# Eight edge streams in the sort and histogram, a four-deep gather ring in the segment max, and GpSimd as gatekeeper of the adjacency

## The chip, the core and the metric

The program runs on one core of one Trainium2 chip. The metric is the device time of one execution in microseconds. A core has five engines with a queue each: TensorE (PE), VectorE (DVE), ScalarE (ACT), GpSimd (POOL) and SyncE (SP). They meet only at semaphores. DMAs are issued from the queues of SP, ACT and POOL; the indirect ones (scatter or gather by a column of row numbers) come from POOL.

## What is computed

A graph of 3125 nodes and 100,000 edges, sorted by destination, goes through four layers. Cut to what matters here:

```
h = relu(layernorm(x));  x = x + L0(h)      # messages by edge type, segment_sum over dst, GRU
h = relu(layernorm(x));  x = x + L1(h)      # edge attention:
    e1, e2 = (efeat @ W_msg) * h[src],  (efeat @ W_attn) * h[src]        # [E, 16, 16]
    m = segment_max(e2, dst);  ex = exp(e2 - m[dst])
    x += segment_sum(e1 * ex / segment_sum(ex, dst)[dst], dst).sum(1)
h = relu(layernorm(x));  x = x + L2(h)      # four graph convolutions with edge weights
h = relu(layernorm(x));  x = x + L3(h)      # sheaf layer with reflections
```

The kernel makes no use of the order in which the edges come: it sorts them itself by destination block.

## The kernel before

The nodes lie in NB = 25 blocks of 128. The kernel is a chain of stages, each a `Block` with a barrier at its end, so the stages add up. Within a stage the order on each engine is the order in which the code is written; loops are `Fori` loops of the hardware, and buffers are mostly two deep, picked by `h = n % 2`.

**Sort.** The 100,000 edges lie as EP = 125 partitions by EC = 800 columns. The columns are cut into NS = 4 streams of SC = 200 columns, and one step takes one column of each stream, 4 x 125 edges. `histogram` counts edges by destination: at each step DVE makes two one-hot tiles (`hot_lo`, 128 wide for each stream, L216, and `hot_hi`, 25 wide, L218) and PE multiplies them into a count. `rank_and_scatter` then gives each edge its slot in the sorted table. Per step s, with two buffers h:

- SP loads two rows for all partitions, `key_row` and `hi_row` (L325, L326), once DVE has released the buffer (`row_used`, after `same` of step s-2).
- DVE runs `one_hots` of step s+1 (L335, L337, then L340, which needs the loaded `hi_row`), and after it `place` of step s: one `same` operation for each stream (L347, needs `key_row`), the release of the row buffer, `picked` (L353), `base` (L355), three small ones and `row_i` (L365).
- PE looks up the counters (`found`, L401) and advances them (`next_ps`, L405). ACT copies the counters (L386) and the records of the step (`staged`, L388).
- POOL waits for `staged` and `row_i` and issues one indirect DMA for each stream, 125 records each (L421), 800 in all. `staged` and `row_i` of step s wait until the DMAs of step s-2 have landed (`sent`).

**Segment max.** After the sort the edges lie in NT = 832 tiles of 128 slots. `segment_max` takes HB = 4 tiles a turn, 208 turns. POOL gathers the node rows of four tiles into `ring`, two turns deep (the helper `gather`, L1257). It waits for `idx`, four columns of row numbers that DVE copies for turn n+2 at the start of turn n (L1331), after `held` says that ACT has read the ring's half. PE turns the gathered rows (`src_ps`, L1403), ACT copies them (`src_t`, L1373; `held`, L1374), PE widens them (L1412) and forms `net` (L1417), ACT copies (`src_w`, L1379), DVE multiplies (`logit`, L1350), scans twice (`run`, L1355), makes `hot` (L1244) and folds the last turn's result into `top` (L1339). PE's order in a turn is: sources and logits of turn n+1, `back` of n (L1430), `best` of n (L1438).

**Adjacency.** `adjacency` takes NT2 = 1408 tiles, eight a turn, 176 turns. DVE makes one-hot and weighted tiles (L635 to L641, six operations); PE adds three products for each tile into PSUM at a column read from `m.table` (L679); ACT copies finished groups out and clears them (`evac`, L658 and L660). Before each tile PE waits for `evac` to reach a number that it reads from the same table; 16 numbers are loaded for a turn. POOL has nothing to do in this stage.

## Time and profile before

| | us |
|---|---|
| median of 3 runs | 8465.72 (8461.97 to 8473.73) |
| the profiled execution | 8461.1 |
| its span, first to last instruction | 8459.0 |
| histogram, 112 to 282 | 170 |
| sort with the histogram's tail, 282 to 1663 | 1381 |
| segment max, 2935 to 4131 | 1196 |
| adjacency, 5500 to 6130 | 630 |

The stages are read off the timeline by the first and last instruction of their lines. Of the span, DVE is busy 73%, PE 69%, POOL 53% and ACT 19%, but no engine is the limit all the way: the stages have different ones. In the rows below, "idle before" is the time that the engine waited ahead of an instruction, and the arrow names what it waited for; "issue" is waiting for nothing that the profile shows.

### The profile page before, as it was taken

Reading aid. Unit: us, or ns where it says so; the run is one execution under the profiler, and the core shown is the slowest. Engines: PE = TensorE matmul, PEld = TensorE weight load, DVE = VectorE, ACT = ScalarE, POOL = GpSimd, SP = SyncE. Lnnn points to the kernel's source line nnn. Section 1 sums busy time; section 2 is a strip of 40 time slices with the busy share of each in tenths; the row PEclk is TensorE's granted clock in tenths of the full one; section 3 lists DMA queues with packets and bytes.
Section 4 is the critical chain, followed back from the end, with each engine's and each line's share of the span. In section 5 each row is a group of like instructions: output and inputs, shape, how many; then the busy total and the mean of one; then the engine's idle time right before and its main releaser. Section 6 shows DMA issues by size and latency. Waiting matters only on the chain. (4 is left out here: it accounts for less than half of the span.)

```text
span 8459.0 us, 123102 instructions
## 1 busy us (share of the span) xinstructions
PE 5854.0 (69%) x33625; PEld 3950.5 (47%) x33626; DVE 6136.2 (73%) x12788; ACT 1635.2 (19%) x2872; POOL 4450.0 (53%) x4142
## 2 busy tenths in 40 slices
PE   3433333347444477777699999466559699999999
PEld 1333333236444455555455555255424366666555
DVE  5766666547333399999899999889900188888898
ACT  0011111001010144444222222034100022222000
POOL 0377767567777577777477777300000177777100
PEclk9999999955555599999899999677879755555899
DMA  2122222233111233333411111022065311111000
GB/s 97 32 52 53 52 51 52 43 108 70 38 36 38 37 79 80 80 80 79 54 44 43 43 44 43 13 94 99 31 253 205 148 31 32 32 32 32 3 0 1
DMA packets 487779, 514.79 MB, mean 61 GB/s; under 512 B 259365, under 2 KB 389805, under 8 KB 477106
## 3 DMA queue, kind: packets, MB, share of 16 engines
q1 hardware_dynamic: 344198, 446.65, 16.9%
q0 software_dynamic: 132160, 43.97, 6.5%
q10 hardware_dynamic: 11232, 21.73, 0.8%
q8 instruction: 109, 1.79, 0.1%
q14 instruction: 80, 0.66, 0.0%
HBM read 415.02 MB, written 95.99 MB: 60 GB/s over the span
## 5 line engine op out<-in xcount | busy, mean ns | idle before, releaser
L1257 POOL DMA_INDIRECT sh_ring<-node,sh_idx x832 | 856.8, 1030 | 1535.4 <-DVE sh_idx L1895 1277.6
L421 POOL DMA_INDIRECT slots<-rank_staged,rank_row_i x800 | 952.0, 1190 | 414.7 <-issue 210.1
L1507 POOL DMA_INDIRECT slots<-sm_rec,sm_row x832 | 900.9, 1083 | 361.8 <-issue 208.8
L1257 POOL DMA_INDIRECT mx_ring<-node,mx_idx x832 | 861.1, 1035 | 398.2 <-issue 239.5
L919 POOL DMA_INDIRECT mid_ring<-typed,mid_idx x832 | 873.5, 1050 | 258.7 <-issue 253.2
L401 PE MATMUL rank_found<-rank_next_sb,rank_hot_hi_t 25*125 25x128 f32 x1600 | 407.3, 431 | 840.3 <-ACT rank_next_sb L386 825.0
L1617 PE MATMUL sm_sums<-sm_both,sm_hot 128*128 128x512 f32 x1664 | 787.1, 595 | 0.4 <-issue 0.2
L401 PEld LDWEIGHTS rank_found<-rank_next_sb,rank_hot_hi_t 25*125 25x125 f32 x1600 | 353.6, 321 | 890.3 <-DVE rank_hot_hi_t L340 890.3
L1124 PE MATMUL mid_sums<-mid_ring,mid_hot_d 128*128 128x17 f32 x1664 | 391.7, 375 | 455.9 <-DMA mid_ring<-typed,mid_idx 443.5
L1124 PEld LDWEIGHTS mid_sums<-mid_ring,mid_hot_d 128*128 128x128 f32 x1664 | 383.3, 312 | 472.6 <-issue 472.6
L2135 PE MATMUL srl_sums<-srl_outer,srl_hot_lo 128*128 128x400 f32 x1664 | 560.9, 500 | 7.4 <-DVE srl_outer L2117 7.4
L679 PE MATMUL adj_sums<-adj_heavy,adj_hot 128*128 128x128 bf16 x4224 | 378.8, 253 | 234.9 <-issue 87.8
L1355 DVE TENSOR_TENSOR_SCAN mx_run<-mx_far,mx_run,mx_logit 128x512 f32<-128x512 f32 x414 | 509.1, 1271 | 21.5
L1438 PE MATMUL mx_best<-mx_run_e,mx_hot 128*128 128x256 f32 x1664 | 422.1, 397 | 48.4 <-ACT mx_run_e L1388 48.0
L679 PEld LDWEIGHTS adj_sums<-adj_heavy,adj_hot 128*128 128x128 bf16 x4224 | 313.9, 114 | 301.2 <-issue 272.4
L2135 PEld LDWEIGHTS srl_sums<-srl_outer,srl_hot_lo 128*128 128x128 f32 x1664 | 316.9, 191 | 252.3 <-DVE srl_outer L2117 9.1
L2035 PE MATMUL sh_hid_ps<-sh_ends_t,mlp 32*128 32x512 f32 x416 | 392.9, 1096 | 54.5 <-ACT sh_ends_t L1988 54.5
L1575 ACT ACTIVATE sm_both<-sm_net_a 128x512 f32<-128x512 f32 x416 | 248.5, 597 | 938.4 <-PE sm_net_a L1604 938.4
L340 DVE TENSOR_SCALAR rank_hot_hi_t<-rank_hi_row,iota_col 25x500 f32<-25x500 f32 x200 | 117.2, 586 | 401.2 <-DMA rank_hi_row<-hi_rows 401.2
L1037 DVE COPY mid_ring<-fields 128x8 f32<-128x8 f32 x104 | 18.9, 181 | 501.7 <-PE mid_sums L1126 501.7
L1617 PEld LDWEIGHTS sm_sums<-sm_both,sm_hot 128*128 128x128 f32 x1664 | 283.3, 190 | 209.8 <-issue 200.8
L1681 DVE TENSOR_TENSOR agg<-c_sums,dinv_row 128x3200 f32<-128x3200 f32 x4 | 14.0, 3492 | 502.3 <-PEq L1720 502.3
(403 smaller groups left out, 13634.0 us busy)
## 6 DMA issues: line engine op xcount, KB each, us to landing
strips<-near SPq DMA_DIRECT2D x76, 1600.0 KB, 10.8
mx_far<-far_row SPq DMA_DIRECT2D x208, 256.0 KB
rank_key_row<-key_rows SPq DMA_DIRECT2D x200, 244.1 KB
near<-adj_whole SPq DMA_DIRECT2D x175, 256.0 KB, 2.0
sm_low<-low_row SPq DMA_DIRECT2D x208, 128.0 KB
sh_low<-low_row SPq DMA_DIRECT2D x104, 256.0 KB, 3.3
feat_t<-mid_out ACTq DMA_DIRECT2D x104, 204.0 KB
mx_feat<-feat_t SPq DMA_DIRECT2D x208, 102.0 KB
```

The lines of the kernel that those rows point to most:

```text
L401: last = nc.tensor.matmul(found[h][:, j, :], hot_hi_t[:, h, j, :], next_sb[:, h, j * P:(j + 1) * P], start=True, stop=True, skip_group_che ...
L421: pool.indirect_dma_start(m.slots, bass.IndirectOffsetOnAxis(ap=row_i[:, h, j:j + 1], axis=0), staged[:, h, j, :], None).then_inc(sent[h], 16)
L679: last = nc.tensor.matmul(sums[:, bass.ds(at[2 * j], P)], hot[:, h, j // 2, :, j % 2], heavy[:, h, k, j // 2, :, j % 2], start=False, stop ...
L919: pool.indirect_dma_start(ring[:, n % DEEP, j, 0:D], None, m.typed, bass.IndirectOffsetOnAxis(ap=idx[:, t:t + 1], axis=0)).then_inc(gather ...
L1124: nc.tensor.matmul(sums[:, bass.ds(blocks[j // 2] * K17, K17)], hot_d[:, h, j, :], ring[:, n % DEEP, j, 0:K17], start=False, stop=True, sk ...
L1257: pool.indirect_dma_start(ring[:, h, j, :], None, table, bass.IndirectOffsetOnAxis(ap=idx[:, h, j:j + 1], axis=0)).then_inc(part, 16)
L1355: last = nc.vector.tensor_tensor_scan(run[:, h, c, :], far[:, h, :], logit[:, c, :], before, ALU.add, ALU.max)
L1438: last = nc.tensor.matmul(best[:, k, :], hot[:, h, 2 * k + j, :], run_e[:, h, 2 * k + j, :], start=j == 0, stop=j == 1, skip_group_check=True)
L1507: pool.indirect_dma_start(m.slots2, bass.IndirectOffsetOnAxis(ap=row2[:, t:t + 1], axis=0), rec2[:, t, :], None).then_inc(ordered, 16)
L1617: last = nc.tensor.matmul(sums[r % 2][:, :], hot[:, h, 2 * (r % 2) + j, :], both[:, r % 2, j].rearrange("q a c -> q (a c)"), start=j == 0, ...
L2035: nc.tensor.matmul(hid_ps[:, c:c + 512], m.mlp1[:, :], ends_t[:, c:c + 512], start=True, stop=True).then_inc(hp_s, 1)
L2135: last = nc.tensor.matmul(sums[:, 0:NB * D], hot_lo[:, h, j, :], outer[:, h, j, :], start=False, stop=True, skip_group_check=True)
```

## The change

NS goes from 4 to 8, so a step of the histogram and the sort takes 8 x 125 edges and there are 100 steps. In `segment_max` the ring is four turns deep, the row numbers of all tiles are copied once, POOL's loop is written out and waits for `held` of turn n-4, and the loops of ACT and PE have bodies of four turns. In `adjacency` POOL reads the `evac` numbers, waits for them and counts tiles free on a new semaphore `freed`; PE waits for that and loads only the eight columns. The table is split into two rows for it.

```
-NS = 4
+NS = 8
...
-                dve.wait_ge(sent[h], i * 64 + 16)
+                dve.wait_ge(sent[h], i * 16 * NS + 16)
...
+        @block.gpsimd
+        def _(pool):
+            def turn(q, h):
+                n = 2 * q + h
+                _, cleared_by = nc.values_load_multi_w_load_instructions(
+                    m.table[0:1, 1, bass.ds(n * BT, BT)], engines=[mybir.EngineType.Pool], min_val=0,
+                    max_val=(NB - 1) * (WIDTH_SLOTS + 1), skip_runtime_bounds_check_because=COUNTED)
+                for j in range(BT):
+                    pool.wait_ge(evac, cleared_by[j] & 511)
+                    pool.sem_inc(freed, 1)
+
+            batches(pool, total, 1, 1, turn)
...
-                    pe.wait_ge(evac, at[2 * j + 1] & 511)
+                    pe.wait_ge(freed, n * BT + j + 1)
...
+    DEEP = 4
-        idx, ring = sb("idx", [P, 2, HB], I32), sb("ring", [P, 2, HB, W40])
+        idx, ring = sb("idx", [P, NT], I32), sb("ring", [P, DEEP, HB, W40])
...
-            gather(nc, m, pool, m.node40, idx, ring, idx_s, gathered, HB, HT // 2)
+            pool.wait_ge(idx_s, 1)
+            for n in range(HT):
+                if n >= DEEP:
+                    pool.wait_ge(held, n - DEEP + 1)
+                for j in range(HB):
+                    t = n * HB + j
+                    pool.indirect_dma_start(ring[:, n % DEEP, j, :], None, m.node40,
+                                            bass.IndirectOffsetOnAxis(ap=idx[:, t:t + 1], axis=0)).then_inc(gathered[n % DEEP], 16)
...
-                if inside(n + 2):
-
-                    dve.wait_ge(held, n + 1)
-                    indices(n + 2, h)
...
+            nc.vector.tensor_copy(idx[:, :], m.fields[:, :, SRC]).then_inc(idx_s, 1)
             nc.vector.memset(m.top[:, :, :], 0.0).then_inc(cleared, 1)
```

What the program issues at the places in question follows. First the loop body of POOL in the sort, two steps; `rec_in` stands for `staged`, `at_row` for `row_i`.

```order
-L421 DMA slots<-rank_staged,rank_row_i 106496x24 [waits rank_rec_in0,rank_at_row0]
-L421 DMA slots<-rank_staged,rank_row_i 106496x24 x3
-L421 DMA slots<-rank_staged,rank_row_i 106496x24 [waits rank_rec_in1,rank_at_row1]
-L421 DMA slots<-rank_staged,rank_row_i 106496x24 x3
...
+L424 DMA slots<-rank_staged,rank_row_i 106496x24 [waits rank_rec_in0,rank_at_row0]
+L424 DMA slots<-rank_staged,rank_row_i 106496x24 x7
+L424 DMA slots<-rank_staged,rank_row_i 106496x24 [waits rank_rec_in1,rank_at_row1]
+L424 DMA slots<-rank_staged,rank_row_i 106496x24 x7
```

Between two waits POOL now has eight indirect DMAs to issue and not four; their number over the sort stays 800.

Second, DVE at the start of a turn of the segment max, before (semaphores are named here by the first stage that used their slot: `rank_sent0` is `held`, `hist_used_d0` is `run_s`, `hist_step` and `hist_counted` are `net_s` and `src_w_s`):

```order
L1331 ISA [waits rank_sent0]
L1331 COPY mx_idx<-fields 128x4
L1240 REGISTER_ALU [waits hist_step,hist_counted]
L1350 TENSOR_TENSOR mx_logit<-mx_net,mx_src_w 128x1024 [waits hist_used_d0]
L1351 ISA
L1355 SCALAR_TENSOR_TENSOR mx_run<-mx_far,mx_run,mx_logit 128x512 [waits hist_used_d1,rec_keys]
```

and now (`hist_used_d0` and `hist_used_d1` are `net_s` and `src_w_s`, `hist_hot_d0` is `run_s`):

```order
L1267 REGISTER_ALU [waits hist_used_d1,hist_used_d0]
L1378 TENSOR_TENSOR mx_logit<-mx_net,mx_src_w 128x1024 [waits hist_hot_d0]
L1379 ISA
L1383 SCALAR_TENSOR_TENSOR mx_run<-mx_far,mx_run,mx_logit 128x512 [waits hist_hot_d1,rec_feat_in]
L1383 SCALAR_TENSOR_TENSOR mx_run<-mx_far,mx_run,mx_logit 128x512
```

The copy and its wait for `held` are gone from the turn, and nothing else moved.

Third, PE in a turn of the adjacency, before (`hist_used_d0` is `hot_s`, `hist_counted` is `evac`):

```order
L672 TENSOR_LOAD table
L675 REGISTER_ALU
L677 REGISTER_ALU [waits hist_used_d0]
L679 ISA [waits hist_counted]
L679 MATMUL adj_sums<-adj_heavy,adj_hot 128x128 x3
```

and what POOL does now in a turn (`hist_used_d0` is here `evac`):

```order
L673 TENSOR_LOAD table
L677 REGISTER_ALU
L677 REGISTER_ALU [waits hist_used_d0] x7
L1241 REGISTER_ALU [waits hist_used_d0]
```

POOL has some ten instructions a turn, and a wait ahead of each tile. On PE the count stays the same: a register operation, a wait and three matmuls a tile, the wait now on `freed`.

## Rows read from the trace of the kernel before

**Rows 1.** Busy time by stage: window, length, PE, PEld, DVE, ACT, POOL, PEclk, DMA share, GB/s.

```profile
112.00:282.00 170.00, 121.92 (x802) 66.28 (x802) 165.82 (x403) 0.00 (x0) 0.00 (x0) 1.00 0.00 0
282.00:1663.00 1381.00, 519.46 (x2410) 421.04 (x2410) 883.90 (x3418) 159.39 (x400) 953.21 (x802) 1.00 0.24 51
2935.00:4131.00 1196.00, 922.94 (x4958) 598.61 (x4958) 1064.88 (x1446) 569.63 (x1035) 861.10 (x832) 0.98 0.37 77
5500.00:6130.00 630.00, 392.76 (x4240) 319.04 (x4240) 576.31 (x1065) 202.25 (x350) 0.00 (x0) 0.81 0.19 75
```

**Rows 2.** Timeline, DVE in the histogram: start, duration, engine, line, operation.

```profile
200.13 0.69 DVE L216 TENSOR_TENSOR hist_hot_lo<-lo_f,iota_row 125x512 bf16<-125x512 f32 x1
201.80 0.69 DVE L216 TENSOR_TENSOR hist_hot_lo<-lo_f,iota_row 125x512 bf16<-125x512 f32 x1
```

**Rows 3.** Groups by line, a one-hot of twice the width: busy us, mean ns, idle before.

```profile
L1038 DVE TENSOR_TENSOR mid_hot_s<-mid_lo,iota_row 128x1024 bf16<-128x1024 bf16 x104 | 126.8, 1219 | 0.0
```

**Rows 4.** Timeline of one sort step, with the idle time and its releaser.

```profile
804.01 1.18 POOL L421 DMA_INDIRECT slots<-rank_staged,rank_row_i  x1 [1.39 <-DVE rank_row_i L365]
...
807.04 0.33 DVE L347 SCALAR_TENSOR_TENSOR rank_same<-rank_key_row,key_f,below 125x125 f32<-125x125 f32 x1
...
812.51 0.64 DVE L340 TENSOR_SCALAR rank_hot_hi_t<-rank_hi_row,iota_col 25x500 f32<-25x500 f32 x1 [1.93 <-DMA rank_hi_row<-hi_rows]
```

**Rows 5.** Half a microsecond of a row load in the sort (columns as rows 1).

```profile
804.00:804.50 0.50, 0.00 (x0) 0.00 (x0) 0.00 (x0) 0.00 (x0) 0.49 (x1) 1.00 0.36 106
```

**Rows 6.** Waits of the sort stage: us in total, times, longest.

```profile
DVE rank_hot_hi_t L340 <- DMA rank_hi_row<-hi_rows: 401.2, 200, 4.7
POOL slots L421 <- DVE rank_row_i L365: 181.4, 134, 2.1
```

**Rows 7.** The scatter: its group, and its min/median/max ns with first and last start.

```profile
L421 POOL DMA_INDIRECT slots<-rank_staged,rank_row_i x800 | 952.0, 1190 | 414.7 <-issue 210.1 <-DVE rank_row_i L365 181.4 <-ACT rank_staged L388 23.1
...
L421 POOL DMA_INDIRECT slots<-rank_staged,rank_row_i x800: 1172/1178/1339, 308.3 to 1659.5; - x160
```

**Rows 8.** Timeline of the segment max, from one pair of turns.

```profile
3501.06 0.38 PE L1403 MATMUL mx_src_ps<-ident_bf,mx_ring 128*48 128x128 bf16 x4 [0.34 <-DMA mx_ring<-node,mx_idx]
...
3504.93 0.94 POOL L1257 DMA_INDIRECT mx_ring<-node,mx_idx  x1 [0.78 <-DVE mx_idx L1331]
3505.45 2.46 DVE L1355 TENSOR_TENSOR_SCAN mx_run<-mx_far,mx_run,mx_logit 128x512 f32<-128x512 f32 x2
3506.17 1.31 POOL L1257 DMA_INDIRECT mx_ring<-node,mx_idx  x1 [0.31 <-issue]
...
3506.43 0.38 PE L1403 MATMUL mx_src_ps<-ident_bf,mx_ring 128*48 128x128 bf16 x4
...
3512.24 0.38 PE L1403 MATMUL mx_src_ps<-ident_bf,mx_ring 128*48 128x128 bf16 x4 [0.50 <-DMA mx_ring<-node,mx_idx]
```

**Rows 9.** The gather and the transposes of its rows: group; then min/median/max ns, first and last start.

```profile
L1257 POOL DMA_INDIRECT mx_ring<-node,mx_idx x832 | 861.1, 1035 | 398.2 <-issue 239.5 <-DVE mx_idx L1331 158.7
...
L1257 POOL DMA_INDIRECT mx_ring<-node,mx_idx x832: 938/944/1947, 2935.2 to 4121.2; - x167
...
L1403 PE MATMUL mx_src_ps<-ident_bf,mx_ring x832: 216/218/314, 2941.5 to 4129.5; 128*48 128x128 bf16 x167
```

**Rows 10.** Ten microseconds near the end of the segment max (columns as rows 1).

```profile
4090.00:4100.00 10.00, 5.85 (x24) 3.87 (x24) 7.03 (x11) 2.91 (x5) 5.64 (x6) 0.83 0.93 48
```

**Rows 11.** Adjacency, 30 us beside ACT's evictions and 30 us without (columns as rows 1).

```profile
5560.00:5590.00 30.00, 18.89 (x213) 15.84 (x211) 28.12 (x53) 13.83 (x24) 0.00 (x0) 0.82 0.25 96
...
6040.00:6070.00 30.00, 16.66 (x221) 12.54 (x219) 28.85 (x55) 0.00 (x0) 0.00 (x0) 1.00 0.00 0
```

**Rows 12.** Waits of the adjacency: us in total, times, longest.

```profile
PE adj_sums L679 <- issue: 87.8, 70, 2.3
PE adj_sums L679 <- ACT adj_sums L660: 78.4, 57, 2.1
...
DVE adj_now L635 <- PE adj_sums L679: 35.1, 72, 1.2
```

More of the change, by code:

```diff
@@ L261, in _ @@
                                     ALU.min).then_inc(step, 1)
-            dve.wait_ge(step, 17)
+            dve.wait_ge(step, 13 + NS)
             nc.vector.tensor_copy(m.pair[:, :], blk_f[:, :].rearrange("o (t a) -> o t a", a=2)[:, :, 0])
@@ L285, in _ @@
             nc.tensor.matmul(small[:, 64:64 + NB], tot[:, :], m.ident[0:NB, 0:NB], start=True, stop=True).then_inc(mm, 1)
-            pe.wait_ge(step, 16)
+            pe.wait_ge(step, 12 + NS)
             h = NT // 2
@@ L391, in _ @@
         def _(pe):
-            nc.tensor.matmul(next_ps[:, :], m.ident[0:NB, 0:NB], m.first[:, :, :].rearrange("p j l -> p (j l)"),
-                             start=True, stop=True, skip_group_check=True).then_inc(seeded, 1)
+            firsts = m.first[:, :, :].rearrange("p j l -> p (j l)")
+            for c in range(0, NS * P, 512):
+                last = nc.tensor.matmul(next_ps[:, c:c + 512], m.ident[0:NB, 0:NB], firsts[:, c:c + 512], start=True, stop=True,
+                                        skip_group_check=True)
+            last.then_inc(seeded, 1)
             for h in range(2):
@@ L423, in _ @@
             for h in range(2):
-                pool.wait_ge(sent[h], turns * 64 + 16)
+                pool.wait_ge(sent[h], turns * 16 * NS + 16)
 def weights(nc, a, m):
@@ L587, in adjacency @@
         sums = ps("sums", [P, 8 * 512])
-        names = ("rec_in", "step", "now_s", "near_s", "hot_s", "done", "evac", "copied", "cleared")
-        rec_in, step, now_s, near_s, hot_s, done, evac, copied, cleared = map(sem, names)
+        names = ("rec_in", "step", "now_s", "near_s", "hot_s", "done", "evac", "copied", "cleared", "freed")
+        rec_in, step, now_s, near_s, hot_s, done, evac, copied, cleared, freed = map(sem, names)
         saved = [sem(f"saved{k}") for k in range(GROUPS)]
@@ L672, in turn @@
                 _, at = nc.values_load_multi_w_load_instructions(
-                    m.table[0:1, bass.ds(n * BT, BT), :].rearrange("o t k -> o (t k)"), engines=[mybir.EngineType.PE], min_val=0,
+                    m.table[0:1, 0, bass.ds(n * BT, BT)], engines=[mybir.EngineType.PE], min_val=0,
                     max_val=(WIDTH_SLOTS - 1) * P, skip_runtime_bounds_check_because=COUNTED)
@@ L676, in turn @@
                 for j in range(BT):
-                    pe.wait_ge(evac, at[2 * j + 1] & 511)
+                    pe.wait_ge(freed, n * BT + j + 1)
                     for k in range(3):
-                        last = nc.tensor.matmul(sums[:, bass.ds(at[2 * j], P)], hot[:, h, j // 2, :, j % 2], heavy[:, h, k, j // 2, :, j % 2], start=False,
+                        last = nc.tensor.matmul(sums[:, bass.ds(at[j], P)], hot[:, h, j // 2, :, j % 2], heavy[:, h, k, j // 2, :, j % 2], start=False,
                                                 stop=True, skip_group_check=True)
@@ L1229, in batches, with fours @@
         body(n // 2, n % 2)
+def fours(eng, total, body):
+    for j in range(4):
+        body(0, j)
+    with eng.Fori(0, total - 2) as i:
+        for j in range(4):
+            body(i + 1, j)
+    for j in range(4):
+        body(total - 1, j)
 def inside(n, total=HT):
@@ L1302, in segment_max @@
         back, best = [ps("back0", [P, 2, 256]), ps("back1", [P, 2, 256])], ps("best", [P, 2, 256])
-        gathered, loaded = [[sem("gathered0")], [sem("gathered1")]], [sem("loaded0"), sem("loaded1")]
+        gathered, loaded = [sem(f"gathered{k}") for k in range(DEEP)], [sem("loaded0"), sem("loaded1")]
         names = ("idx_s", "src_s", "src_t_s", "wide_s", "src_w_s", "net_s", "logit_s", "run_s", "back_s", "run_e_s", "hot_s",
@@ L1359, in turn @@
                     keep(n - 1)
+            nc.vector.tensor_copy(idx[:, :], m.fields[:, :, SRC]).then_inc(idx_s, 1)
             nc.vector.memset(m.top[:, :, :], 0.0).then_inc(cleared, 1)
             dve.wait_ge(cleared, 1)
-            for h in range(2):
-                indices(h, h)
             batches(dve, HT, 3, 3, turn)
@@ L1369, in _, with sources @@
         def _(act):
-            def sources(q, h):
-                n = 2 * q + h
+            def sources(n, k):
                 act.wait_ge(src_s, n + 1)
-                nc.scalar.copy(src_t[:, h], src_ps[:, :]).then_inc(src_t_s, 1)
-                nc.scalar.copy(m.held[:, bass.ds(n * HB, HB), :], ring[:, h, :, 0:D]).then_inc(held, 1)
+                nc.scalar.copy(src_t[:, k % 2], src_ps[:, :]).then_inc(src_t_s, 1)
+                nc.scalar.copy(m.held[:, bass.ds(n * HB, HB), :], ring[:, k, :, 0:D]).then_inc(held, 1)
             def widened(n):
@@ L1391, in _, with sources @@
             widened(0)
[L1392 removed]
+            fours(act, HT // 4, turn)
         @block.tensor
         def _(pe):
[L1396 to L1399 removed]
+            def sources(q, k):
+                n = 4 * q + k
+                pe.wait_ge(gathered[k], (q + 1) * 16 * HB)
                 wait(pe, src_t_s, n)
@@ L1413, in logits @@
                 last.then_inc(wide_s, 1)
-                pe.wait_ge(loaded[h], (q + 1) * 32)
+                pe.wait_ge(loaded[h], (2 * q + k // 2 + 1) * 32)
                 wait(pe, logit_s, n)
@@ L1443, in _ @@
             logits(0, 0)
-            batches(pe, HT, 1, 1, turn)
+            fours(pe, HT // 4, turn)
 def split_top(nc, m):
@@ L2244, in build @@
             rb = on(scope)
-            m.table, m.marks = rb("table", [1, NT2, 2], I32), rb("marks", [1, NB, 8], I32)
+            m.table, m.marks = rb("table", [1, 2, NT2], I32), rb("marks", [1, NB, 8], I32)
             bucket_table(nc, m)
```

36 lines of the change are left out of this document (15 added, 21 removed).

## The prediction, made before the run

> **What bounds the kernel now.** First the busy time by stage [rows 1], because the engines' shares of the whole span average over stages with different limits. The change touches four stages: histogram (170 us), sort (1381), segment max (1196) and adjacency (630). The others are left as they are, and barriers stand between stages, so what a stage gains the kernel gains.
>
> *Histogram.* DVE is busy 165.8 of 170 us: it is the bound. Two steps take 201.80 - 200.13 = 1.67 us [rows 2].
>
> *Sort.* No engine is full; POOL, with 953 of 1381 us, is nearest. So the waits. POOL waits 181 us for `row_i`, and DVE waits 401 us, at all 200 steps, for the loaded `hi_row` [rows 6]. One step shows the loop [rows 4]: the last `same` ends at 807.37 and releases the row buffer, SP loads the rows anew, `hi_row` is there at 812.51 (5.14 us after the release, 1.93 us of it plain waiting on DVE), `hot_hi_t` takes up to 0.64, four `same` follow at 0.27 each, and the buffer is released again: 5.14 + 0.5 + 1.1 = 6.7 us a step. 1351 us from the first scatter to the last [rows 7] over 200 steps are 6.76. This loop is the bound, with POOL close behind: four scatters at 1.19 us and 0.3 us before each (1.19 is the mean [rows 7], 0.3 is what stands before an indirect DMA that waits for nothing [rows 8]) are 5.96.
>
> *Segment max.* DVE is busy 1065 of 1196 us, PE 923. Here the engines wait for each other in turn. PE starts its turns at 3501.06, 3506.43 and 3512.24: 5.37 us to a start that waits for nothing, 5.81 to one that waits 0.50 for the gather, whose POOL waited 0.78 for DVE's `idx` [rows 8]. The whole stage runs at (4129.4 - 2941.5)/207 = 5.74 a turn [rows 9], more than the 5.6 of such a pair, because POOL now and then needs 1.9 us for a gather in place of 0.94 [rows 9] and because near the end the DMA engines are 93% busy at a mere 48 GB/s [rows 10].
>
> *Adjacency.* DVE is busy 576 of 630 us. It makes 53 operations (8.8 turns) in 30 us beside ACT's evictions and 55 (9.2 turns) without them [rows 11]: DVE is the bound, and loses 35 us to a late PE, which lost 78 us to ACT [rows 12].
>
> **Histogram, part by part.** 100 steps of twice the width. A one-hot of 512 takes 0.69 [rows 2], one of 1024 1.22 [rows 3]: 0.53 more. `hot_hi` grows by 100 elements, by the same rate 0.10. A step is then 0.84 + 0.53 + 0.10 = 1.47, the stage 147 us in place of 167: **-20**. Its tail has wider operations and four more additions, and the seeding product is doubled: I charge **+4**, from 0 to 8; that work stands alone, so nothing hides it.
>
> **Sort.** The number of scatters stays at 800, and their cost on POOL too. What changes is what a round trip of the row load pays for: eight scatters, not four. Two limits compete.
> POOL: 8 x 1.49 = 11.9 us a step.
> The loop of the row load: 586 KB in place of 293. While it runs the DMA shows 106 GB/s at a share of 0.36 [rows 5], so the added 293 KB cost 2.8 us: 5.14 + 2.8 = 7.9, plus `hot_hi_t` 0.5 to 0.9 and eight `same` 2.2, is 10.6 to 11.0. The DVE work that lies beside the load (picked, base, small ones, two one-hots, about 4.6) is covered. That is under POOL's 11.9, by 1 us. ACT and PE round trips grow to some 7 us and are covered too, and `sent` of step s-2 comes some 8 us before POOL wants step s.
> So POOL becomes the bound: 799 x 1.49 = 1191 in place of 1351: -160. Two limits that lie so near disturb each other a little: +3 (none to 10). The first scatter comes later: two row loads in a row, each 2.9 longer, and the wider chain behind them (same 1.1, picked and base 0.5 each): +8. Sum **-149**.
> Ends: 1.48 a scatter, -157. At the other end the load's whole 5.14 doubles, not its data part alone (a rival, below).
>
> **Segment max.** The `idx` copy, its wait and POOL's wait for it go; nothing of it comes back but one copy of 832 numbers ahead of the stage. Next is PE's own chain: 5.37 a turn [rows 8]. POOL needs 4 x 1.035 + 4 x 0.29 = 5.29 [rows 9], now without a partner to wait for: almost as much. I take 5.42. Gathers of 1.9 us vanish in a ring three turns ahead. Near the end the DMA engines stay full, which a ring can't change; of some nine turns at 6.9 I keep 8 us over 5.42, and 2 for the first turns at PE's lower clock. 207 x 5.42 + 10 = 1132 against 1188: -56. POOL also starts 5 us earlier, as `idx` is copied before the memset of `top` and not after: -4 net of the longer copy. **-60**; with 5.37 a turn -70, with 5.6 (a rival) -23. POOL's loop written out means no other cost that a row shows: the ends of the turns in its present loop cost the same 0.3.
>
> **Adjacency.** PE keeps its count of instructions and loads 8 numbers, not 16. That saves at most a part of its 88 us of "issue" [rows 12], and PE is not the bound. Each tile for which PE waited for ACT now has a hand-over through POOL on the way. The trace has no POOL instruction in this stage, so bounds: below, 35 us, all that DVE waits for PE, if a lighter PE made it good; above, POOL's whole 0.78 us before a gather that waited for `idx` [rows 8], which holds the waiting itself, at each of PE's 57 waits for ACT [rows 12], 45 us. A semaphore alone is nearer to the bottom; 0.15 us each is **+8**.
>
> **Sum**: -20 + 4 - 149 - 60 + 8 = **-217**. 8461.1 - 217 = 8244 for an execution like the profiled one, which lies 4.6 under the median: **8248**. What is hidden or small (table split, ACT's wider copies) I cost at nothing: in each case the engine has over a third of the stage idle.
>
> **Rivals.**
> *The row load stays the bound.* If issue and landing grow with the size as well, 10.3 + 0.8 + 2.2 = 13.3 us a step, 1330 for the sort: -13 for -149, total 8384. For it: SP's row loads come from rows of 500 bytes, and DMA engines are shared with a denser scatter. Against: the load's fixed part. Partly so (12.3 a step): 8285.
> *POOL and DVE collide in the segment max.* Inside a scan of 1.2 us a gather took 1.31 in place of 0.94 [rows 8], others up to 1.95. Today POOL's start is tied to DVE's `idx`, before the scans; untied, a gather may begin anywhere in them. Half a scan lost a turn: 4 x 1.25 + 0.6 = 5.6, -23 for -60: 8285. A whole scan, 6.2, would be +101 for -60, 8409.
> The Trainium skill, "SBUF — State Buffer", "Who interferes with whom", says that a DVE operation with two inputs in SBUF and a GpSimd operation that reads SBUF exclude each other for the whole instruction. The 1.31 agrees in kind; by that rule at its hardest the whole-scan figure would hold.
> *The kernel gets slower: POOL paces the adjacency.* POOL has eight waits, eight register operations and a load a turn. If each costs the 0.3 us that stand before POOL's DMAs, a turn is 17 x 0.3 = 5.1 us in place of 3.5, 176 turns +280 for +8: total 8520. It decides from 3.5/17 = 0.2 us an instruction. Against: POOL's waits at step ends in the sort cost nothing over the 0.3.
> *The change does nothing* in the sort, because POOL's pace is not 1.49 when DVE never idles: it would need 1.69 a scatter, above all but a few; the longest is 1.34 [rows 7].
>
> **Chances.** Forecast (8215 to 8280) 0.62; collision in the segment max 0.17; row load, wholly or partly, 0.13; slower 0.03; better than the forecast, with a gain in the adjacency too, 0.05. The range takes in the bounds of the segment max, the partial row load, and a gain of 20 in the adjacency: 8195 to 8325. A difference of 0.2% (17 us) is about what a measurement can tell. Faster 0.95, same 0.02, slower 0.03.
>
> **What would show it.** Histogram: DVE's `hot_lo` every 1.47 us. Sort: POOL's wait for `row_i` near zero, 1.5 us from scatter to scatter, DVE waiting for `hi_row` still but without anyone waiting for DVE. Segment max: no gather waits for `idx`; the transposes every 5.4 us; PE's wait for the gather small. If POOL's mean gather is over 1.1 us and PE waits for the ring, the collision is real. Adjacency: DVE's wait for PE at 35 us or a little more; POOL well ahead. The prediction is wrong if POOL still waits for `row_i` at most steps, or if the adjacency grows by more than 50 us.

## The result, and the profile after

| | before | after |
|---|---|---|
| median us | 8463.84 (8461.23 to 8473.73, 4 runs) | 8240.52 (8215.09 to 8245.35, 4 runs) |
| span of the profiled execution | 8459.0 | 8242.4 |
| histogram | 170 | 149 |
| sort with the histogram's tail | 1381 | 1280 |
| segment max | 1196 | 1149 |
| adjacency | 630 | 583 |

The ratio is 0.9728, with a 95% interval of 0.9706 to 0.9750: 223 us by the medians, 217 by the two spans. The four stages give 21 + 101 + 47 + 47 = 216, so the rest of the kernel did not move. The forecast was 8248. The total is almost exact, but two of its terms are off by 44 and 55 us in opposite directions, and that is what the experiments are about.

The stages after (window, length, PE, PEld, DVE, ACT, POOL, PEclk, DMA share, GB/s); they answer to [rows 1]:

```profile
112.00:261.00 149.00, 106.40 (x804) 76.54 (x804) 145.10 (x205) 0.00 (x0) 0.00 (x0) 1.00 0.00 0
261.00:1541.00 1280.00, 477.53 (x2412) 424.62 (x2412) 759.43 (x2520) 128.59 (x200) 999.91 (x802) 1.00 0.26 55
2811.00:3960.00 1149.00, 913.24 (x4962) 592.96 (x4963) 1040.73 (x1241) 575.69 (x1036) 857.84 (x832) 0.98 0.39 81
5329.00:5912.00 583.00, 336.62 (x4240) 249.96 (x4240) 567.71 (x1064) 201.52 (x350) 0.00 (x0) 0.98 0.21 81
```

**Histogram.** Timeline of DVE, against [rows 2]:

```profile
199.55 1.22 DVE L216 TENSOR_TENSOR hist_hot_lo<-lo_f,iota_row 125x1024 bf16<-125x1024 f32 x1
200.68 0.35 DVE L218 TENSOR_TENSOR hist_hot_hi<-hi_f,iota_row 125x200 bf16<-125x200 f32 x1
200.96 1.22 DVE L216 TENSOR_TENSOR hist_hot_lo<-lo_f,iota_row 125x1024 bf16<-125x1024 f32 x1
```

A step takes 200.96 - 199.55 = 1.41 us, over the stage 1.43.

**Sort.** The scatter's group and its smallest, median and longest duration, against [rows 7], and below them two waits of the stage, against [rows 6]:

```profile
L424 POOL DMA_INDIRECT slots<-rank_staged,rank_row_i x800 | 998.7, 1248 | 265.5 <-issue 260.0 <-ACT rank_staged L388 3.7 <-DVE rank_row_i L365 1.8
...
L424 POOL DMA_INDIRECT slots<-rank_staged,rank_row_i x800: 1175/1184/2410, 295.1 to 1536.1; - x160
```

```profile
DVE rank_row_i L365 <- DMA slots<-rank_staged,rank_row_i: 308.7, 78, 5.2
DVE rank_hot_hi_t L340 <- DMA rank_hi_row<-hi_rows: 101.1, 31, 8.9
```

POOL waits 1.8 us for `row_i` in place of 181, and but for 5.5 us all of its idle time is "issue": POOL is the bound, as forecast. Scattering takes 1536.1 - 295.1 = 1241 us, 110 less than before. But the mean scatter has grown from 1190 to 1248 ns, while the median has hardly moved; 74 of the 800 take over 1.5 us, the longest 2.41. The timeline shows which:

```profile
901.08 1.18 POOL L424 DMA_INDIRECT slots<-rank_staged,rank_row_i  x1 [0.30 <-issue]
902.22 0.17 DVE L365 SCALAR_TENSOR_TENSOR rank_row_i<-rank_pos 125x8 int32<-125x8 int32 x1 [5.10 <-DMA slots<-rank_staged,rank_row_i]
902.34 1.23 DVE L335 TENSOR_TENSOR rank_hot_lo<-lo_f,iota_row 125x1024 bf16<-125x1024 f32 x1
902.57 2.26 POOL L424 DMA_INDIRECT slots<-rank_staged,rank_row_i  x1 [0.30 <-issue]
...
905.14 1.21 POOL L424 DMA_INDIRECT slots<-rank_staged,rank_row_i  x1 [0.31 <-issue]
```

A scatter that begins at 902.57, inside `hot_lo` (902.34 to 903.57), ends 2.26 us later and not 1.18. Counted over the stage, 88 scatters begin inside `hot_lo`, with a mean of 1.73 us, and 73 of the 77 that take over 1.4 us are among them. The earlier in `hot_lo` a scatter begins, the longer it takes: 2.29 us on the mean at 0.1 to 0.2 us after its start, 1.53 at 0.9 to 1.0. So it waits for `hot_lo` to end, and ends itself 1.05 to 1.27 us later. (The eight that begin in its first 0.03 us take 1.18 and don't wait.) They meet so often because something ties them: DVE waits 5.10 us for the landing of an earlier scatter, then writes `row_i` and goes straight on to `hot_lo`, in the rhythm of the scatters.

In the kernel before, 96 scatters begin inside `hot_lo` too, but each in its last 0.15 us, and they take 1.18 us:

```profile
809.72 0.69 DVE L335 TENSOR_TENSOR rank_hot_lo<-lo_f,iota_row 125x512 bf16<-125x512 f32 x1 [0.34 <-issue]
810.28 1.18 POOL L421 DMA_INDIRECT slots<-rank_staged,rank_row_i  x1 [0.63 <-issue]
```

**Segment max.** The transposes run from 2818.9 to 3957.9, 1139.0 us against 1188 [rows 9]. Gather and pace in 800 us of the middle (3019 to 3819), and under it the end of the stage (the columns of the windows as above):

```profile
L1360 POOL DMA_INDIRECT mx_ring<-node,mx_idx x600 | 617.8, 1030 | 182.9 <-issue 180.5 <-ACT held L1400 2.4
```

```profile
3820.00:3880.00 60.00, 49.29 (x272) 32.30 (x270) 56.27 (x68) 30.56 (x56) 45.97 (x47) 1.00 0.38 87
3880.00:3920.00 40.00, 26.98 (x125) 17.39 (x124) 28.20 (x35) 14.85 (x27) 30.21 (x29) 0.83 0.88 54
3920.00:3958.00 38.00, 20.38 (x96) 13.69 (x96) 17.86 (x22) 10.74 (x19) 3.78 (x4) 0.78 0.59 48
```

600 gathers in 800 us are 1.33 us each, 5.33 a turn, and that is just a gather (1.030) and what stands before it (0.30): POOL has hardly any other idle time (2.4 us) and sets the pace. Then the end: 78 us in which PE does 221 matmuls. At the pace of the 60 us before (272) that is 49 us. The DMA engines are 88% busy there with less to move than before.

**Adjacency.** The products run from 5344.9 to 5909.4, 564.5 us; before it was 5517.1 to 6128.0, 610.9. Its waits, against [rows 12]:

```profile
PE adj_sums L695 <- DVE adj_heavy L644: 129.1, 93, 2.1
PE adj_sums L695 <- POOLq L678: 114.9, 83, 1.6
```

DVE has no wait for PE left (35.1 us before), PE waits for DVE. A turn takes (5904.6 - 5341.5)/175 = 3.22 us, which is DVE's own work, and the granted clock is 0.98 where it was 0.81 [rows 1].

### The profile page after: what moved, and what is told of

It is laid out like the page before. It is cut to its first block and busy times, and to the rows that moved or that the text cites. A ratio compares the mean times of both kernels' runs of the same rounds, so it can differ in the third digit from the quotient of the medians.

```text
span 8242.4 us, 120531 instructions
## 1 busy us (share of the span) xinstructions
PE 5734.8 (70%) x33629; PEld 3891.4 (47%) x33630; DVE 5955.1 (72%) x11485; ACT 1609.0 (20%) x2672; POOL 4496.5 (55%) x4143
## 3 DMA queue, kind: packets, MB, share of 16 engines
q8 instruction: 111, 1.82, 0.1%
## 5 line engine op out<-in xcount | busy, mean ns | idle before, releaser
L424 POOL DMA_INDIRECT slots<-rank_staged,rank_row_i x800 | 998.7, 1248 | 265.5 <-issue 260.0
L404 PE MATMUL rank_found<-rank_next_sb,rank_hot_hi_t 25*125 25x128 f32 x1600 | 374.3, 422 | 764.0 <-ACT rank_next_sb L386 748.5
L695 PE MATMUL adj_sums<-adj_heavy,adj_hot 128*128 128x128 bf16 x4224 | 322.7, 222 | 244.0 <-DVE adj_heavy L644 129.1
L695 PEld LDWEIGHTS adj_sums<-adj_heavy,adj_hot 128*128 128x128 bf16 x4224 | 245.0, 98 | 323.2 <-issue 275.5
L2068 PE MATMUL sh_v_ps<-mlp,sh_hid 128*128 128x32 f32 x1664 | 374.5, 401 | 0.0
```

Of the source, the lines that this page charges most:

```text
L404: last = nc.tensor.matmul(found[h][:, j, :], hot_hi_t[:, h, j, :], next_sb[:, h, j * P:(j + 1) * P], start=True, stop=True, skip_group_che ...
L424: pool.indirect_dma_start(m.slots, bass.IndirectOffsetOnAxis(ap=row_i[:, h, j:j + 1], axis=0), staged[:, h, j, :], None).then_inc(sent[h], 16)
L695: last = nc.tensor.matmul(sums[:, bass.ds(at[j], P)], hot[:, h, j // 2, :, j % 2], heavy[:, h, k, j // 2, :, j % 2], start=False, stop=Tru ...
```

## The experiments

`e1` to `e4` ran on a chip where the kernel before takes 9395 us, `e9` and `e10` on one where it takes 9419, and `e5` to `e8` on one where it takes 8450, close to the first comparison. On the first two, engines stop in the segment max and other stages for "issue" and "remote", up to 10.8 us at a time; what makes them is not resolved. Ratios are therefore taken within a batch, and stages are compared by their rows. The old products of the adjacency span 610.7 to 611.3 us in `before`, `e1` and `e5`. The scatters of the unchanged eight-stream sort vary more: 1241.0 us after the change, 1241.7 in `e1`, 1239.5 in `e3`, 1236.6 in `e8` and 1224.8 in `e6`.

### Which edit brings what

`e1_sort_only` and `e2_adjacency_only` take one part of the change each over into the kernel before; `e5_ring_only` takes the third.

```
 e1:  -NS = 4          +NS = 8
 e2:  bucket_table and adjacency of the change
      -rb("table", [1, NT2, 2], I32)   +rb("table", [1, 2, NT2], I32)
 e5:  segment_max of the change
```

> The kernel before with eight streams in the histogram and the sort, and nothing else of the change. If the stages are independent, histogram and sort take what they take in the changed kernel: the one-hot every 1.43 us, 1241 us from the first scatter to the last, and the other stages stay as before; total about 8464 - 25 - 110 + 13 (the later last scatter is in these) = 8340 +- 10. If part of the gain of the changed kernel elsewhere came from the sort (another order of the slots), segment max or adjacency move by over 5 us.

> The kernel before with the adjacency of the change (POOL reads the evac numbers and hands tiles to PE by freed; PE loads eight numbers a turn) and nothing else. If the 46 us there come from this edit: products from first to last 565 us and not 611, DVE waits for PE for nothing, granted clock in the stage 0.98 and not 0.81, total about 8418. If they come from the other stages (a denser program ahead, another clock history), the stage stays at 611 and the total at 8464.

> Only the four-deep ring of the segment max is taken over into the kernel before; histogram, sort and adjacency stay at four streams and at the old release. My theory: the stage is set by VectorE at about 5.3 to 5.4 us a turn, and the deeper ring takes the waits for a landed gather away; on a chip like the one of the first two traces the row of the turned gathers would span 1139 us in place of 1188, the ratio would be 0.994 and the other stages would not move. Rival (collision): if GpSimd's gathers had grown beside VectorE's two-operand work, their mean would be over 1.1 us and the stage would not shorten; the trace of the changed kernel shows 1031 ns, so I expect this to fail. Second rival: where the landings are slower, as in the four experiments before, the ring is used up by the landings, and the stage is set by them before and after: ratio 0.985 to 1.0 with gather waits left on TensorE or on GpSimd's hold.

| | ratio | 95% interval | the stage |
|---|---|---|---|
| e1 | 0.9895 | 0.9857 to 0.9933 | scatters span 1241.7 us, mean 1249 ns, as after |
| e2 | 0.9938 | 0.9916 to 0.9961 | products 564.5 us, as after |
| e5 | 0.9950 | 0.9935 to 0.9966 | transposes 1165.4 us, after 1139.0 |

The adjacency in `e2`, 584 us of its trace, and its waits:

```profile
6142.00:6726.00 584.00, 336.81 (x4240) 250.00 (x4240) 567.71 (x1064) 201.41 (x350) 0.00 (x0) 0.98 0.21 81
```

```profile
PE adj_sums L692 <- DVE adj_heavy L641: 127.7, 93, 1.5
PE adj_sums L692 <- POOLq L675: 116.7, 83, 2.5
```

Both agree with the changed kernel to within 2 us: the 46 us in the adjacency come from its own edit and from nothing else in the change. So do the long scatters from the eight streams. The expectation of `e5` failed: the ring alone is worth half of what its stage gained, 22.5 us of 49. The three ratios multiply to 0.978 where the whole change has 0.973; half of that gap is the 26 us that the ring lacks here, the rest lies within the intervals. Its gathers in the middle of the stage:

```profile
L1344 POOL DMA_INDIRECT mx_ring<-node,mx_idx x580 | 624.5, 1077 | 176.7 <-issue 176.7
```

1.077 + 0.30 four times is 5.51 a turn, against 5.33. POOL paces the stage here too, with the same ring, but its gathers are 4% longer. In the changed kernel three of a turn's four take 0.95 us and one 1.13 to 1.61:

```profile
3301.91 2.46 DVE L1383 TENSOR_TENSOR_SCAN mx_run<-mx_far,mx_run,mx_logit 128x512 f32<-128x512 f32 x2
3302.57 1.38 POOL L1360 DMA_INDIRECT mx_ring<-node,mx_idx  x1 [0.30 <-issue]
```

and in `e5` one at the same place takes 1.79:

```profile
3302.24 2.46 DVE L1367 TENSOR_TENSOR_SCAN mx_run<-mx_far,mx_run,mx_logit 128x512 f32<-128x512 f32 x2
3302.49 1.79 POOL L1344 DMA_INDIRECT mx_ring<-node,mx_idx  x1 [0.30 <-issue]
```

How far a scan has got when the gather begins decides its length. The two scans shown together as x2 start 1.20 us apart. After the change the first ends at 3303.20, the gather at 3303.95; in `e5` the scan ends at 3303.53, the gather at 3304.28. So it is for all of them: the 150 long gathers of the 800 us after the change, the 144 of `e5` and the 135 of the kernel before all begin inside a scan (a DVE operation with both inputs in SBUF) and end 0.75 us after it, where the others take 0.95 in all. They begin 0.77 us into the first scan after the change (median) and 0.55 us in `e5`. The gathers cost 0.34 and 0.53 us a turn by this, and 4 x (0.944 + 0.30) = 4.98 and these make the two paces, 5.33 and 5.51. Why the same code settles at one distance with eight streams and at another with four wasn't tried, and stays open.

### The long scatters of the sort

`e4_iota_in_psum`: the changed kernel, in which ACT copies the counting row to PSUM once and both one-hots of the sort compare against the copy. DVE does the same work in the same time, with one of its two inputs outside SBUF.

```
+        iota_ps, iota_s = ps("iota_ps", [EP, P]), sem("iota_s")
...
-                 m.iota_row[0:EP, None, :].to_broadcast([EP, NS, P]), ALU.is_equal)
+                 iota_ps[:, None, :].to_broadcast([EP, NS, P]), ALU.is_equal)
...
+            nc.scalar.copy(iota_ps[:, :], m.iota_row[0:EP, :]).then_inc(iota_s, 1)
```

> The changed kernel, with the row of column numbers that the sort's one-hots are compared against held in PSUM and not in SBUF, so that these two operations of DVE read one operand from SBUF and one from PSUM. Theory A, DVE shuts POOL out while it reads two operands from SBUF: the scatters of 2.3 us beside the wide one-hot (1.23 us) vanish, the mean scatter falls from 1.25 to about 1.20 us, the sort from 1241 to about 1200 us, total about 8200. Theory B, the long scatter comes from the DMA side (it starts as the last scatter of two steps before lands): nothing changes.

Ratio 0.9668 (0.9633 to 0.9703); `e3`, which ran beside it and has the sort of the changed kernel, has 0.9779. Of the 105 us between the two medians only 40 are the scatters (1239.5 and 1199.6 us); 63 are the slower adjacency of `e3`. Scatter group and durations, and the place that was long before:

```profile
L427 POOL DMA_INDIRECT slots<-rank_staged,rank_row_i x800 | 957.3, 1197 | 264.6 <-issue 257.9 <-ACT rank_staged L391 5.2 <-DVE rank_row_i L366 1.5
...
L427 POOL DMA_INDIRECT slots<-rank_staged,rank_row_i x800: 1175/1181/1653, 294.3 to 1493.9; - x160
```

```profile
899.15 1.22 DVE L336 TENSOR_TENSOR rank_hot_lo<-lo_f,rank_iota_ps 125x1024 bf16<-125x1024 f32 x1 [0.35 <-issue]
899.32 1.18 POOL L427 DMA_INDIRECT slots<-rank_staged,rank_row_i  x1 [0.30 <-ACT rank_staged L391]
```

The scatter again begins inside `hot_lo`, which takes 1.22 us as it did, and now takes 1.18; so do all 80 that begin inside it (mean 1.18, in place of 1.73). The mean of all is down from 1248 to 1197 ns, no scatter is over 1.65 us, and the scatters span 1199.6 us in place of 1241. DVE still waits for the landings as it did (262 us here, 309 there), so it is the second input in SBUF that holds POOL up, and not the landing or the load of the DMA engines. The stage's gain in `e4`, `e7` and `e10` (1197 to 1200 us) against the five spans above is 25 to 44 us. The Trainium skill, "SBUF — State Buffer", "Who interferes with whom", says that a DVE operation with two SBUF inputs and a GpSimd operation that reads SBUF exclude each other, and that one with a single SBUF input does not contend: this pair of runs agrees with both halves, with 2.26 and 1.18 us. The same section infers that a `tensor_tensor` does not stall GpSimd's issue of DMAs; `hot_lo` is one, and the 2.26 us say that it does, so the measurement decides.

### What slowed the adjacency before

The change does two things to PE there: it loads 8 numbers a turn in place of 16, and it waits for a constant in place of a register's value. Its count of instructions is the same. `e3_load_sixteen` puts the table and PE's load back and keeps the hand-over through POOL, whose own load is then of every second number. `e8_wide_load` was meant to leave POOL's load alone and to widen only PE's, and its expectation says so. But the kernel that ran as `e8` is line for line that of `e3`: it is a repetition on another chip, and it separates nothing.

```
 e3 and e8
     -m.table[0:1, 1, bass.ds(n * BT, BT)]      (POOL)
     +m.table[0:1, bass.ds(n * BT, BT), 1]
...
     -m.table[0:1, 0, bass.ds(n * BT, BT)]      (PE)
     +m.table[0:1, bass.ds(n * BT, BT), :].rearrange("o t k -> o (t k)")
```

> The changed kernel, but the table is laid out as before and PE loads all sixteen numbers of a turn again, of which it uses eight; POOL still does the waiting. Theory A, PE's sequencer: the time that PE needs between two bursts is mostly this load (1.27 us of idle before a burst at full clock before, with DVE's operands ready); with sixteen numbers it comes back, the stage goes to 595 to 612 us and the granted clock falls. Theory B, the waits: PE was held up by waits whose number came out of a register loaded from the table; these stay with POOL, so the stage stays at 565.

> The changed kernel; only TensorE's sequencer loads 16 numbers a turn of the adjacency products, the 8 it needs and GpSimd's 8, and uses the first 8. GpSimd's own load stays as it is, a row of 8 that lie together. Theory A (the width of TensorE's load was the second bound of the stage before): the products span 600 us or more in place of 564.5, TensorE starts its bursts 1 us or more after its operands are ready, and its clock falls below 0.9. Theory B (the width costs nothing; the experiment with the interleaved table was slow for GpSimd's load of every second number, and the kernel before for its 8 waits against a register): 560 to 570 us, clock 1.0, as in the changed kernel.

`e3` has a ratio of 0.9779 (0.9751 to 0.9808), `e8` 0.9813 (0.9793 to 0.9833). The products take 627.9 and 629.6 us, more than `e3`'s theory A allowed (595 to 612) and more than the 611 of the kernel before. The stage in `e8`, then its waits:

```profile
5321.50:5967.00 645.50, 399.51 (x4238) 326.17 (x4239) 578.08 (x1064) 201.59 (x348) 0.00 (x0) 0.78 0.19 73
```

```profile
PE adj_sums L695 <- POOLq L678: 242.0, 173, 2.4
DVE adj_now L638 <- PE adj_sums L695: 53.3, 103, 1.7
...
PE adj_sums L695 <- DVE adj_heavy L644: 4.0, 3, 2.0
```

The wait booked on "POOLq" is real here. The trace also keeps a record of each sequencer's loads and semaphore instructions, which the views shown leave out. POOL's load of eight numbers takes 0.57 us in the changed kernel (0.66 on the mean) when they lie side by side, and 1.82 us or more (2.02 on the mean) when they are every second one. With the eight hand-overs at 0.16 us each and the loop's own instructions that makes a turn of POOL 3.60 us in `e8`, and in it POOL stands still for an `evac` once, for 0.5 us. In 101 of 174 turns PE starts its first tile within 0.05 us of POOL's release. So `e3` and `e8` are slow because POOL paces the stage, and they can't tell what PE's load costs. In the changed kernel POOL's release lies at least 3 us ahead of PE's first tile in every turn, and there the 83 waits booked on POOLq are not waits for POOL.

What slowed the stage before is in the same records. A turn of PE's sequencer in its parts, means in us:

| | before | after | e8 | e9 |
|---|---|---|---|---|
| load from the table | 1.24 | 0.67 | 1.25 | 0.66 |
| from there to the first tile's matmuls | 0.26 | 0.63 | 0.37 | 0.36 |
| first to eighth tile | 1.50 | 1.49 | 1.50 | 2.87 |
| from there to the next load | 0.49 | 0.43 | 0.48 | 0.53 |
| turn | 3.48 | 3.22 | 3.59 | 4.42 |

Before, none of the 174 turns holds a wait of over 0.04 us for DVE's operands, and the eight waits for `evac` cost next to nothing: the first to eighth tile take 1.50 us against a register, 1.49 against a constant. PE's sequencer is always busy, and its 3.48 us are the stage's turn. The waits that the profile books there on ACT [rows 12] are its sequencer's. The change takes 0.57 us out of the load; 0.38 us of it come back as waiting for DVE, whose turn of 3.22 is now the bound. So it is the width of the load (theory A), shown by `before`, `e2` and the changed kernel, and the register waits (theory B) are out. A load of 16 numbers takes 1.11 us where nothing is evicted and 1.29 on the mean beside evictions; one of 8, 0.59 and 0.69.

A timeline shows the same from the side of the matmuls. Before, without an eviction near:

```profile
6042.69 1.85 PE L679 MATMUL adj_sums<-adj_heavy,adj_hot 128*128 128x128 bf16 x24 [1.27 <-issue]
6046.26 1.83 PE L679 MATMUL adj_sums<-adj_heavy,adj_hot 128*128 128x128 bf16 x24 [1.72 <-issue]
6049.38 1.83 PE L679 MATMUL adj_sums<-adj_heavy,adj_hot 128*128 128x128 bf16 x24 [1.28 <-issue]
```

after:

```profile
5853.43 1.85 PE L695 MATMUL adj_sums<-adj_heavy,adj_hot 128*128 128x128 bf16 x24 [1.39 <-DVE adj_heavy L644]
5856.65 1.81 PE L695 MATMUL adj_sums<-adj_heavy,adj_hot 128*128 128x128 bf16 x24 [1.37 <-DVE adj_heavy L644]
```

Before, the starts are 3.57 and 3.12 us apart, 3.35 on the mean, and PE waits for nothing but its own sequencer. DVE's turn of 3.22 lies below that: PE was the bound, by a little. After, the starts are 3.22 apart, and it is DVE's `heavy` that ends the wait. Beside the evictions the longer loads add to the 3.35. The longer turn goes with a lower granted clock. A hundred microseconds beside the evictions, of `e8` and of the changed kernel:

```profile
5420.00:5520.00 100.00, 62.61 (x663) 52.95 (x660) 88.47 (x164) 41.90 (x73) 0.00 (x0) 0.74 0.24 94
```

```profile
5430.00:5530.00 100.00, 56.93 (x750) 43.13 (x749) 98.95 (x187) 46.44 (x81) 0.00 (x0) 1.00 0.27 105
```

The clock is 0.74 against 1.00, and DVE makes 164 operations against 187. In `e8` a burst takes 2.74 us in place of 1.83 where the clock is low:

```profile
5890.96 2.74 PE L695 MATMUL adj_sums<-adj_heavy,adj_hot 128*128 128x128 bf16 x24 [1.71 <-POOLq L678]
5894.20 1.83 PE L695 MATMUL adj_sums<-adj_heavy,adj_hot 128*128 128x128 bf16 x24 [0.50 <-POOLq L678]
```

The longer burst is not what makes the turn long: PE's sequencer goes from the first to the eighth tile in 1.50 us at a clock of 0.78 and in 1.49 at 0.98, and the burst of 2.74 is followed by the next after 0.50 us.

If only the width counts, the relay through POOL isn't needed: `e9_packed_before` puts address and count of a tile in one number, and PE takes them apart.

```
-                    pe.wait_ge(evac, at[2 * j + 1] & 511)
+                    pe.wait_ge(evac, (at[j] >> 12) & 511)
...
-    last = nc.tensor.matmul(sums[:, bass.ds(at[2 * j], P)], ...
+    last = nc.tensor.matmul(sums[:, bass.ds(at[j] & 3968, P)], ...
```

> The kernel before, and only the adjacency's table is another: address and evacuation count of a tile stand in one number, so TensorE loads 8 numbers a turn in place of 16 and takes them apart with two further register instructions a tile (16 a turn). There is no relay through GpSimd; TensorE waits against a register as before. Theory (the width of the load is what costs, about 65 us over 176 turns, 0.37 us a turn): the products go from 611 to 565 to 580 us, TensorE's clock in the stage goes above 0.9, and the ratio is 0.994 to 0.997, as with the relay. Rival (the relief came from the wait against a constant in place of one against a register, or the register instructions cost as much as the loads): the products stay at 605 us or more and the ratio is 0.999 to 1.001.

The ratio is 1.0155 (1.0133 to 1.0177), slower than before, and the products take 775.8 us. Two of its turns:

```profile
6603.04 3.35 PE L680 MATMUL adj_sums<-adj_heavy,adj_hot 128*128 128x128 bf16 x24 [0.96 <-ACT adj_sums L661]
6607.58 3.38 PE L680 MATMUL adj_sums<-adj_heavy,adj_hot 128*128 128x128 bf16 x24 [1.19 <-ACT adj_sums L661]
```

The theory missed; the rival had the direction (605 us or more), but not the size. The load is as narrow as in the change, but two more register instructions a tile, 0.10 us each, stretch the burst itself to 3.35 us, beyond even the 2.74 of the low clock: 4.41 us a turn, with DVE waiting for PE in 174 turns (193 us). Over the first 620 us of the stage the granted clock is 0.52, for the most part the lower of the two levels (1.2 GHz):

```profile
6180.00:6800.00 620.00, 467.89 (x3337) 262.00 (x3335) 459.62 (x842) 203.01 (x348) 0.00 (x0) 0.52 0.19 74
```

So here PE's sequencer, not its array, sets the pace, as it did before the change: 16 register instructions more cost 0.93 us a turn, although 8 numbers fewer are loaded. The hand-over through POOL is good for exactly this: it takes eight numbers off PE's sequencer and puts nothing on it. It pays only with the table split, so that POOL's numbers too lie side by side.

### The slow end of the segment max

`e6_spread_holes`: unused slots of the sorted list name spread rows; in the changed kernel they all name row 0.

```
+ nc.vector.tensor_scalar(hv[:, :, FIELDS + SRC], m.iota_col[:, 0:1].to_broadcast([P, 32]), 24.0, None, ALU.mult).then_inc(hole_s, 1)
+ nc.vector.tensor_scalar(hv[:, :, FIELDS + TIX], m.iota_col[:, 0:1].to_broadcast([P, 32]), 192.0, None, ALU.mult).then_inc(hole_s, 1)
```

> The changed kernel, but an unused slot of the sorted list names a source row of its own partition (24 times the partition's number, and the type index likewise) and not row 0. Unused slots weigh nothing, so the output does not change; the gathers of the last turns read 128 different rows where they read one row 128 times. My theory: the slow end of the segment max (3880 to 3958 in the changed kernel: 78 us for work that takes 49 us at the pace ahead of it, DMA share 0.88 at 54 GB/s against 0.38 at 87) is the price of reading one address many times. Then the stage ends about 30 us earlier, the DMA share in its last 80 us is that of the stretch ahead, and the total falls by 25 to 60 us against the changed kernel, since other passes gather the same slots. Rival: the slow end belongs to other transfers that start there; then nothing moves, and the tail keeps its share of over 0.8.

The transposes take 1110.0 us, 29 less than in the changed kernel, as expected. The ratio is 0.9710 (0.9682 to 0.9739); against the 0.9728 of the changed kernel the intervals overlap, so the gain in the total isn't resolved, and by the stage it is 29 us and not up to 60. Its sort was 16 us shorter as well, with the same code: 59 scatters of over 1.4 us in place of 77. The last 77 us:

```profile
3825.00:3865.00 40.00, 33.07 (x182) 21.55 (x180) 37.56 (x46) 20.37 (x38) 30.86 (x31) 1.00 0.36 88
3865.00:3902.00 37.00, 30.14 (x165) 19.69 (x166) 34.82 (x43) 19.33 (x35) 26.12 (x26) 1.00 0.32 84
```

The DMA share stays at 0.32 to 0.36, and the longest gather from issue to landing is 4.2 us, where it was 19.0 (10.4 before the change, and 17.0 in `e5` with the deeper ring alone; that more gathers in flight make the difference is an inference). What I had taken in the prediction for full DMA engines, which a ring can't help, was many reads of one row.

### Together

`e7_both` has both edits on top of the change; `e10_packed_both` is `e7` with the packed table for the relay.

> The changed kernel with two edits at once: the sort's one-hots compare against a copy of the counting row in PSUM, and the unused slots name spread rows. If the two act in different stages they add up: the sort's scatters span 1200 us in place of 1241, and the segment max loses its slow end; about 70 us under the changed kernel, ratio to the kernel before 0.963 to 0.966 if the chip is as the one of the first four experiments, 0.964 on one like the first. If the spread rows do nothing, this kernel equals the one with the copy in PSUM alone (0.967).

> The kernel with the counting row in PSUM and the spread unused slots (0.9648 of before), with the packed table of the run above in place of GpSimd's relay. If packing does all that the relay does, the products take 565 us again and the ratio stays 0.963 to 0.967. If the relay is also worth something by itself (a wait less on TensorE's sequencer), the products take 575 us or more and the ratio is 0.966 or higher. VectorE's own work sets 3.21 us a turn either way, so neither can bring the stage under 560 us.

`e7`: 8150.74 us (8150.44 to 8152.82, 4 runs), ratio 0.9648 (0.9632 to 0.9664), the best of all. Its scatters span 1198.3 us, its transposes 1107.0. The two add up, as they act in different stages. `e10`: 0.9877 (0.9858 to 0.9897), with products of 775.8 us as in `e9`. The second expectation (575 us or more) holds, but not for its reason, a wait less on PE: it is the register instructions again.

## Why the prediction came out right, point by point

- **Histogram, -20 + 4.** A step takes 1.43 where 1.47 was worked out; 0.04 over 100 steps is the difference. The stage lost 21 us, and of the tail's +4 nothing shows apart in the sort's window.
- **Sort, -149: right in mechanism, too large.** POOL is the bound, the row load is covered: `hi_row` is still waited for in 31 of 100 steps, but no scatter waits for it, so the rival "row load stays the bound" is out. The term that was mis-sized is "799 x 1.49 = 1191": 1.49 rests on 1.19 a scatter [rows 7], measured where the scatters that began inside `hot_lo` began in its last 0.15 us, and where `hot_lo` was 0.69 us long and not 1.23. Measured 1.248 + 0.30, 1241 us. 800 x 0.058 = 46 us are what the collision costs, and `e4` gives 41 of them back against the changed kernel. The rule was on the table, as a rival for the segment max; it belonged at every place where the change lets POOL run freely beside a two-input operation of DVE. The first scatter, put at +8, came 13 us earlier, since the histogram ahead of it is 21 shorter: relative to that it is 8 later, as said.
- **Segment max, -60.** Measured -49 in the row of transposes, -47 in the stage. The pace was better than the 5.42 taken, 5.33, and the limit is POOL's 5.29 of the text, not PE's 5.37. The collision of the rival is real and was there all along: one gather a turn waits for a scan, in the kernel before as after, and its price stood already in the mean of 1.035 [rows 9]. It is 0.34 us a turn after the change and 0.53 in `e5`, where the rival charged 0.6 and the forecast nothing more. That the distance to the scan did not shrink with the untied ring is luck: nothing in the prediction says where it would settle. The stated sign (a mean gather of over 1.1 us) could not see it. The end was worse: it cost 29 us over the pace where 8 were kept, and `e6` shows why.
- **Adjacency, +8: wrong sign.** Measured -46. The failed step is "PE is not the bound": it was read from DVE's busy share and from the 35 us that DVE waits. But an undisturbed DVE turn is 3.22 us, and the stage ran at (6122.2 - 5513.5)/175 = 3.48; a stage bound by DVE would have run at 3.22. What set the pace was PE's sequencer, with a load of 1.24 us in each turn. The lower end of the term, 35 us, was the wait of DVE alone, and the real gain lies beyond it. The 57 "waits for ACT" that the +8 was multiplied from were no waits for ACT in the sequencer's records, so the hand-over had nothing to delay. The rival on the other side, POOL as the pace, is out in this kernel, where its instructions take 0.08 us and its load 0.66; it came true in `e3` and `e8`, by the load and not by the waits.
- **Sum.** -217 forecast, -217 between the spans. By the stages: sort with the histogram's tail 44 us too much (-145 forecast, -101 measured), adjacency 55 too little, segment max 13 too much, histogram 1 too little. The total is right because errors cancelled, and that is luck.

## What to carry to other kernels

When a change makes GpSimd the bound, price its instructions by those that run beside the other engine, not by the mean of a trace in which it waited; and look for VectorE operations with two SBUF inputs that follow in its rhythm, since moving one shared constant to PSUM gave back 41 us here. Where an engine with runtime addresses issues short matmuls, compare the stage's turn with the busy engine's turn: here the gap of 3.48 to 3.22 us was a sequencer, and there every loaded number and register instruction counts. Lay numbers that one load fetches side by side. And let padding entries point at different rows.

## What the runs showed of the hardware

- A scatter that begins inside a VectorE operation with both inputs in SBUF waits for its end: up to 2.41 us in place of 1.18, with 88 cases at a mean of 1.73; with one input in PSUM, 1.18 (80 cases). A gather that begins inside a scan ends 0.75 us after the scan (150 cases after the change, 144 in `e5`, 135 before).
- TensorE's sequencer loads 8 numbers of a table in SBUF in 0.59 us and 16 in 1.11, so 0.06 us for each number more. The Trainium skill, "Runtime: NRT & Kernel Launch", "Instruction fetch mechanics", gives about 200 ns a register for this instruction; here a number of such a load takes 0.07 us, and the measurement decides.
- GpSimd's load of 8 numbers side by side: 0.57 us; of every second number: 1.82 us or more (`e3`, `e8`).
- A register instruction on TensorE's sequencer between two matmuls: 0.10 us; two more a tile took the burst of 24 matmuls from 1.83 us to 3.35 (`e9`).
- Gathers of 128 rows that all name the same row: up to 19.0 us to land, in place of 4.2, with the DMA share at 0.88 for 54 GB/s.
